# A layer's parameter loads issued one chunk sooner on SyncE, between the value transfers

## Chip, cores and metric
The kernel runs on one core of a Trainium2 chip. The metric is the device time of one execution in microseconds (us). The kernel before takes 7104.73 us, the median of three runs (7095.42 to 7106.72).

## What is computed
One sequence of 2048 tokens, 128 wide, in float32, passes four stages, each added to its input: causal attention with 16 heads of 8, a stack of 6 layers, grouped attention (16 query heads, 4 key groups of 64), and the same stack of 6 layers again with the same parameters. The change lies in the stack. One of its layers, cut to what matters:

```
def attn_layer(x, Wqkv, qs, ksc, Wo):          # 16 heads of 64, window 32
    q, k, v = split(x @ Wqkv)
    q = rotary(l2norm(q) * qs);  k = rotary(l2norm(k) * ksc)
    return local_attention(q, k, v) @ Wo
def ffn_layer(x, g, bln, W1, b1, W2, b2):      # hidden width 341
    xn = layernorm(x) * g + bln
    a, gate = split(xn @ W1 + b1)
    return a * gelu(gate) @ W2 + b2
for i in range(6):
    x = attn_layer(shift_tokens(x), Wqkv[i], q_scale[i], k_scale[i], Wo[i]) + x
    x = ffn_layer(shift_tokens(x), ln_g[i], ln_b[i], W1[i], b1[i], W2[i], b2[i]) + x
```

## The kernel before
A layer of the stack is worked through in 16 chunks of 128 tokens. The feed-forward part works on blocks of 4 chunks. Everything is one software pipeline: every engine runs a function `step` for k = 0 to 15 of each layer, and in one step it does different work for different chunks. On TensorE, step k holds the query and key projection of chunk k (L535 to L537), the value projection and the transposes of chunk k-1 (L542), the scores of chunk k-2 (a mask matmul, L704, then L711), the product of probabilities and values of chunk k-3 (L681), and the output projection of chunk k-4 with the weights `Wo` (L602). Block b enters the feed-forward part when its last chunk c = 4b+3 is through: the gate matmuls with `W1` (L546) run in step c+7, the three value matmuls with `W1` in steps c+8 to c+10 (each counted on `value_mm`), the matmuls with `W2` (L646) in step c+11. Within a step the order on TensorE is: normalisation and first value matmul, output projection (L602), gate matmul, transpose of the probabilities, `W2` matmuls, query projection, L681, L704 and L711, then the transposes and the value projection. The pipeline doesn't drain between layers: steps 0 to 11 of a layer still hold feed-forward work of the last block of the layer before.

Two steps follow from this for each layer's own parameters. `Wo` is last read for the layer before in step 3 (chunk 15) and first read for this layer in step 4 (chunk 0). `W1` is last read for the layer before in step 9 and first read for this layer in step 10. The biases `b1` of the value half are read by `hide` on VectorE (L1155) for the layer before until VectorE's step 10, and for this layer from its step 12. VectorE's step numbers run ahead of TensorE's: the product for this layer meets the chunk that TensorE has in step 11. Each parameter has one buffer, so its load waits until the last read of the layer before is done.

All these loads are issued by SyncE (SP), in program order, from `layer` in `sp_stack`. That function runs over the 16 chunks of a layer. For each chunk c it calls `window_values`, which waits until ScalarE has copied the values V of chunk c out of PSUM (L793, `v_sb`, at the end of TensorE's step c+1) and then issues ten transfers from `V` to `VW` (L456, L458, L460). They feed the L681 matmuls of chunk c, in step c+3. The parameter loads stand between these calls: each has the chunk c before whose `window_values` it is issued, and a wait on the semaphore of the last read. SP waits for both in the order in which they are written. Layer 0 of each call of the stack has its parameters loaded beforehand (`first`), so that the loads in question belong to 5 layers of each of the 2 calls, 10 in all. `load_wo` is one transfer (L422), `load_w1` one (L426), `load_b1` three (L436), `load_w2` three (L431), `load_cols` two (L441), `load_b2` one (L445) and `load_scales` six (L414, L417).

Of the kernel before, what the change touches and what calls it, by code (L numbers as in the profile page):

```python
# [90 lines left out]
def build(nc, A, out, place, stages=("A", "S0", "B", "S1")):  # L91
    n_const = A["shape_constants"].shape[1]
    ctx = ExitStack()
    with ctx:
# [303 lines left out]
        def sp_stack(sp, call):  # L398
            def load_q(layer):
                sp.dma_start(w_raw[0][:, :], A["Wqkv"][bass.ds(layer, 1), :, 0:INNER].rearrange("a p n -> p (a n)"))\  # L400
                  .then_inc(s["wqv_raw_in"], 16)

            def load_k(layer):
                sp.dma_start(w_raw[1][:, :], A["Wqkv"][bass.ds(layer, 1), :, INNER:2 * INNER]
                             .rearrange("a p n -> p (a n)")).then_inc(s["wk_raw_in"], 16)

            def load_v(layer):
                sp.dma_start(w_raw[0][:, :], A["Wqkv"][bass.ds(layer, 1), :, 2 * INNER:3 * INNER]
                             .rearrange("a p n -> p (a n)")).then_inc(s["wqv_raw_in"], 16)

            def load_scales(layer):
                for j, name in enumerate(("q_scale", "k_scale")):
                    row = A[name][bass.ds(layer, 1), :].rearrange("a n -> (a n)")
                    sp.dma_start(qk_scales[:, 2 * j, :], row.partition_broadcast(128))\  # L414
                      .then_inc(s["scales_in"], 16)
                    for x in range(2):
                        sp.dma_start(qk_scales[:, 2 * j + 1, 32 * x:32 * x + 32],  # L417
                                     row[32 - 32 * x:64 - 32 * x].partition_broadcast(128))\
                          .then_inc(s["scales_in"], 16)

            def load_wo(layer):
                sp.dma_start(Wo[:, :, :], A["Wo"][bass.ds(layer, 1), :, :].rearrange("a (j p) n -> p (a j) n", p=128))\  # L422
                  .then_inc(s["wo_in"], 16)

            def load_w1(layer):
                sp.dma_start(W1[:, :], A["W1"][bass.ds(layer, 1), :, :].rearrange("a p n -> p (a n)"))\  # L426
                  .then_inc(s["w1_in"], 16)

            def load_w2(layer):
                for j, (a, n) in enumerate(FT):  # L430
                    sp.dma_start(W2[0:n, j, :], A["W2"][bass.ds(layer, 1), a:a + n, :].rearrange("a p n -> p (a n)"))\  # L431
                      .then_inc(s["w2_in"], 16)

            def load_b1(layer, i):
                for j, (a, n) in enumerate(FT):
                    sp.dma_start(b1[0:n, i, j:j + 1], A["b1"][bass.ds(layer, 1), i * DFF + a:i * DFF + a + n]  # L436
                                 .rearrange("a p -> p a")).then_inc(s["gate_b_in" if i else "value_b_in"], 16)

            def load_cols(layer):
                for j, name in enumerate(("ln_g", "ln_b")):  # L440
                    sp.dma_start(ffn_cols[:, j:j + 1], A[name][bass.ds(layer, 1), :].rearrange("a p -> p a"))\  # L441
                      .then_inc(s["ln_cols_in"], 16)

            def load_b2(layer):
                sp.dma_start(ffn_cols[:, 2:3], A["b2"][bass.ds(layer, 1), :].rearrange("a p -> p a"))\  # L445
                  .then_inc(s["b2_in"], 16)

            def window_values(g, c):
                par = c % 2
                sp.wait_ge(s["v_sb"], START + g + c + 1)  # L450
                sp.sem_inc(s["passed"], 1)
                sp.wait_ge(s["pv_mm"], START + (max(g + c - 1, 0) if isinstance(g, int) else g + c - 1))
                for x in range(2):
                    cols = slice(512 * x, 512 * x + 512)
                    for w in range(1, 4):
                        sp.dma_start(VW[par][64 * x:64 * x + 64, w, :], V[par][32 * w - 32:32 * w + 32, cols])\  # L456
                          .then_inc(s["vs_in"], 16)
                    sp.dma_start(VW[par][64 * x:64 * x + 32, 0, :], V[1 - par][96:128, cols])\  # L458
                      .then_inc(s["vs_in"], 16)
                    sp.dma_start(VW[par][64 * x + 32:64 * x + 64, 0, :], V[par][0:32, cols])\  # L460
                      .then_inc(s["vs_in"], 16)

            def layer(L, following, after):
                first = isinstance(L, int) and L == 0
                g, f = L * NCH + CHUNKS * call, L * NB + BLOCKS * call
                t = (L + DEPTH * call) * 3
                if following is not None:
                    sp.wait_ge(s["w_lo_done"], START + t + 3)
                    load_q(following)
                for c in range(NCH):  # L470
                    if c == NCH - 1 and following is not None:
                        sp.wait_ge(s["w_lo_done"], START + t + 4)
                        load_v(following)
                        if after is not None:
                            sp.wait_ge(s["w_lo_done"], START + t + 5)
                            load_k(after)
                    if c == 3 and not first:
                        sp.wait_ge(s["y_mm"], START + g)
                        load_wo(L)
                    if c == 5:  # L480
                        sp.wait_ge(s["tables_done"], START + TABLES * call + 4 + 16 * L)
                        load_scales(0 if following is None else following)
                    if c == 7 and not first:
                        sp.wait_ge(s["ln_done"], START + norms_before(call) + f)
                        load_cols(L)
                    if c == 8 and not first:
                        sp.wait_ge(s["gelu_done"], START + 3 * f)
                        load_b1(L, 1)
                    if c == 9 and not first:
                        sp.wait_ge(s["value_mm"], START + 3 * f)  # L490
                        load_w1(L)
                    if c == 10 and not first:
                        sp.wait_ge(s["hid_done"], START + 3 * f)
                        load_b1(L, 0)
                    if c == 11 and not first:
                        sp.wait_ge(s["w2_mm"], START + f)
                        load_w2(L)
                    if c == 12 and not first:
                        sp.wait_ge(s["f_done"], START + 2 * f)
                        load_b2(L)  # L500
                    window_values(g, c)
# [21 lines left out]
        def norms_before(call):  # L523

            return (1 + (LN_S0 if call == 0 else LN_S1)) * NB - BLOCKS * call
# [1600 lines left out]
```

## Time and profile before
| | |
|---|---|
| time, median of 3 runs | 7104.73 us |
| the profiled execution: own time / span | 7119.09 / 7117.3 us |
| TensorE matmul busy / weight load busy | 6050.2 us (85%) / 4080.9 us (57%) |
| VectorE busy | 4642.6 us (65%) |
| GpSimd busy | 4252.9 us (60%) |
| ScalarE busy | 3318.6 us (47%) |
| mean granted TensorE clock over the span | 0.89 of full |

The times of the rows below come from the profiled execution. Its span runs from the first to the last instruction, and 1.8 us lie around it. A row of the timeline says when something started, how long it was busy, and in brackets how long its engine had been idle before it and what ended that idle time. The two calls of the stack lie at about 1040 to 3060 us and at about 5110 to 7117 us.

### The profile page before, as it was taken

The page shows a single profiled execution, that of the slowest core. Times are in us where ns is not written, and L with a number is a line of the kernel's source. Part 1 is how long each engine was busy: PE and PEld are TensorE (multiplying, and loading weights), DVE is VectorE, ACT ScalarE, POOL GpSimd, SP SyncE. Part 2 cuts the span into 40 slices and gives each one's busy share as a digit, 9 for nine tenths or more (in the row PEclk, how much of TensorE's full clock was granted, in tenths as well). Part 3 has the DMA queues.
Part 4 walks back from the last instruction along what each step waited for, and adds up shares of the span by engine and source line. Part 5 has one row for each costly group of instructions (what it writes and reads, how often), then busy time and mean ns, then how long its engine had stood idle before and what let it go on. Part 6 is the DMA issues. An engine that isn't in the chain of part 4 may idle for free. (4 is left out here: it accounts for less than half of the span.)

```text
span 7117.3 us, 188486 instructions
## 1 busy us (share of the span) xinstructions
PE 6050.2 (85%) x75387; PEld 4080.9 (57%) x75387; DVE 4642.6 (65%) x5380; ACT 3318.6 (47%) x3775; POOL 4252.9 (60%) x2000
## 2 busy tenths in 40 slices
PE   8989878888888888889889889999688888888887
PEld 4334436666666666655555555555376666666665
DVE  5425528887878887775455445543388787878776
ACT  1342246665656555513333333333366565656554
POOL 0000008777777777616567666667787777777764
PEclk6665569999999999989989989999899999999999
DMA  0000002222222222200000000000122222222221
GB/s 23 1 2 1 1 22 62 67 59 62 59 62 59 64 60 59 53 8 1 1 2 1 1 2 1 1 1 1 31 64 65 57 68 54 67 65 61 57 56 49
DMA packets 187287, 254.59 MB, mean 36 GB/s; under 512 B 59996, under 2 KB 80984, under 8 KB 186200
## 3 DMA queue, kind: packets, MB, share of 16 engines
q1 hardware_dynamic: 186392, 242.02, 13.1%
q8 instruction: 639, 10.47, 0.6%
q14 instruction: 256, 2.10, 0.1%
HBM read 38.98 MB, written 1.57 MB: 6 GB/s over the span
## 5 line engine op out<-in xcount | busy, mean ns | idle before, releaser
L1813 POOL TENSOR_TENSOR XB<-XB,Pb 128x1024 f32<-128x1024 f32 x448 | 1079.3, 2409 | 290.3 <-ACT Pb L1771 265.1
L913 POOL TENSOR_TENSOR sin_qk<-raw_qk,rot 128x512 f32<-128x512 f32 x768 | 1008.9, 1334 | 188.7 <-ACT raw_qk L875 133.1
L1865 DVE TENSOR_REDUCE b_pmax<-slot 128x1 f32<-128x1024 f32 x512 | 621.2, 1223 | 611.5 <-PE slot L1607 611.3
L1771 ACT ACTIVATE Pb<-slot 128x1024 f32<-128x1024 f32 x512 | 504.5, 1024 | 951.7 <-PE slot L1634 880.5
L946 POOL TENSOR_TENSOR inv_norm<-norm2c,minus_half 128x16 f32<-128x16 f32 x192 | 678.2, 3532 | 386.9 <-DVE norm2c L1088 386.9
L929 POOL TENSOR_TENSOR rot_out<-rot_out,sin_qk 128x1024 f32<-128x1024 f32 x192 | 601.2, 3131 | 337.7 <-DVE rot_out L987 336.6
L286 POOL TENSOR_TENSOR rstd<-variance,minus_half 128x4 f32<-128x4 f32 x20 | 19.8, 1008 | 1075.6 <-DVE variance L295 1075.5
L535 PE MATMUL slot<-w_hi,x_hi 128*128 128x512 f32 x1152 | 538.2, 467 | 73.5 <-POOL w_lo L904 43.4
L786 ACT ACTIVATE qT<-slot 128x1024 f32<-128x1024 f32 x192 | 197.1, 1026 | 794.3 <-PE slot L542 794.3
L942 POOL TENSOR_TENSOR inv_norm<-norm2c,minus_half 128x16 f32<-128x16 f32 x192 | 559.0, 2912 | 0.0
L987 DVE TENSOR_TENSOR rot_out<-slot,rot 128x1024 f32<-128x1024 f32 x384 | 467.9, 1219 | 83.5 <-PE slot L542 42.6
L711 PE MATMUL slot<-kT,qT 64*32 64x64 f32 x24576 | 334.6, 229 | 218.4 <-issue 218.3
L1644 PE MATMUL slot<-Pb,Vb 128*64 128x512 f32 x2048 | 494.3, 604 | 1.1 <-ACT Pb L1771 1.1
L542 PE MATMUL slot<-consts,rot_out 128*128 128x128 f32 x3072 | 435.1, 287 | 69.3 <-issue 39.5
L991 DVE TENSOR_TENSOR rot_out<-rot_out,inv_norm 128x1024 f32<-128x1024 f32 x384 | 474.9, 1237 | 6.8 <-POOL inv_norm L942 5.3
L602 PE MATMUL slot<-OT,Wo 128*128 128x128 f32 x3072 | 404.9, 288 | 82.7 <-DMA Wo<-in_Wo 80.0
L536 PE MATMUL slot<-w_lo,x_hi 128*128 128x512 f32 x1152 | 471.4, 409 | 2.6 <-issue 2.6
L537 PE MATMUL slot<-w_hi,x_lo 128*128 128x512 f32 x1152 | 469.6, 408 | 0.0
L711 PEld LDWEIGHTS slot<-kT,qT 64*32 64x32 f32 x24576 | 274.1, 107 | 325.9 <-issue 325.9
L602 PEld LDWEIGHTS slot<-OT,Wo 128*128 128x128 f32 x3072 | 386.5, 203 | 106.7 <-issue 101.8
L542 PEld LDWEIGHTS slot<-consts,rot_out 128*128 128x128 f32 x3072 | 363.8, 147 | 137.7 <-issue 84.0
L1632 PE MATMUL slot<-QA,KA 128*128 128x512 f32 x1024 | 423.6, 414 | 11.3 <-ACT Pb L1771 7.5
(223 smaller groups left out, 13525.8 us busy)
## 6 DMA issues: line engine op xcount, KB each, us to landing
VW<-V SPq DMA_DIRECT2D x1152, 128.0 KB
VW<-V SPq DMA_DIRECT2D x768, 64.0 KB
w_raw<-in_Wqkv SPq DMA_DIRECT2D x36, 512.0 KB, 3.6
Wo<-in_Wo SPq DMA_DIRECT2D x12, 512.0 KB, 4.1
W<-in_W SPq DMA_DIRECT2D x12, 341.0 KB, 3.1
consts<-in_shape_constants SPq DMA_DIRECT2D x1, 2436.5 KB, 8.7
W<-in_W SPq DMA_DIRECT2D x24, 64.0 KB
out<-out_nat SPq DMA_DIRECT2D x2, 512.0 KB, 3.4
```

The source lines that it names most:

```text
L535: pe.matmul(out, x_hi[ring][:, :], w_hi[:, cols], start=True, stop=False)
L542: mm = pe.transpose(o[:, j * 128:(j + 1) * 128], src[:, j * 128:(j + 1) * 128], ident)
L602: mm = pe.matmul(slot[2][:, 512:640], Wo[:, j, :], OT[:, j, :], start=(j == 0), stop=(j == 7))
L711: mm = pe.matmul(slot[3][32 * w:32 * w + 32, col:col + 64], qT[r:r + 64, h // 2, 32 * w:32 * w + 32], kT[r:r + 64, h // 2, 32 * w:32 * w + ...
L913: ins = pool.tensor_tensor(dst[:, :, x, :], src[:, :, 1 - x, :], tab, ALU.mult)
L929: pool.tensor_tensor(rot_out[0][:, :], rot_out[0][:, :], rot_sin[0], ALU.add)\
L942: pool.tensor_tensor(inv_norm[0][:, :], norm2c[0][:, :], minus_half[:, 0:H], ALU.pow)\
L946: pool.tensor_tensor(inv_norm[1][:, :], norm2c[1][:, :], minus_half[:, 0:H], ALU.pow)\
L1644: mm = pe.matmul(slot[3][64 * hh:64 * hh + 64, 0:512], Vb[:, k, :], Pb[:, n % B_RING, 512 * hh:512 * hh + 512], start=(k == 0), stop=(k == ...
L1771: act.activation(Pb[:, n % B_RING, :], slot[n % 2][:, :], ACT.Exp).then_inc(s["b_exp"], 1)
L1813: pool.tensor_tensor(b_sum[:, qb % 2, :], Pb[:, (n - 1) % B_RING, :] if k == 1 else b_sum[:, qb % 2, :], Pb[:, n % B_RING, :], ALU.add).th ...
L1865: dve.tensor_reduce(b_pmax[:, n // 2, n % 2:n % 2 + 1], o[:, :], AX.X, ALU.max).then_inc(s["b_max"], 1)
```

## The change
In `layer` eight conditions change. Each load that stood before the value transfers of chunk c now stands before those of chunk c-1. Their order among themselves, their waits and what they load stay the same. The loads of the projection weights (`load_q`, `load_v`, `load_k`) are not touched.

```diff
@@ -474,28 +474,28 @@
-                    if c == 3 and not first:
+                    if c == 2 and not first:
                         sp.wait_ge(s["y_mm"], START + g)
                         load_wo(L)
-                    if c == 5:
+                    if c == 4:
                         sp.wait_ge(s["tables_done"], START + TABLES * call + 4 + 16 * L)
                         load_scales(0 if following is None else following)
-                    if c == 7 and not first:
+                    if c == 6 and not first:
                         sp.wait_ge(s["ln_done"], START + norms_before(call) + f)
                         load_cols(L)
-                    if c == 8 and not first:
+                    if c == 7 and not first:
                         sp.wait_ge(s["gelu_done"], START + 3 * f)
                         load_b1(L, 1)
-                    if c == 9 and not first:
+                    if c == 8 and not first:
                         sp.wait_ge(s["value_mm"], START + 3 * f)
                         load_w1(L)
-                    if c == 10 and not first:
+                    if c == 9 and not first:
                         sp.wait_ge(s["hid_done"], START + 3 * f)
                         load_b1(L, 0)
-                    if c == 11 and not first:
+                    if c == 10 and not first:
                         sp.wait_ge(s["w2_mm"], START + f)
                         load_w2(L)
-                    if c == 12 and not first:
+                    if c == 11 and not first:
                         sp.wait_ge(s["f_done"], START + 2 * f)
                         load_b2(L)
                     window_values(g, c)
```

## Rows read from the trace of the kernel before

**Rows 1.** The page, part 1: busy time of each engine.
```profile
PE 6050.2 (85%) x75387; PEld 4080.9 (57%) x75387; DVE 4642.6 (65%) x5380; ACT 3318.6 (47%) x3775; POOL 4252.9 (60%) x2000
```

**Rows 2.** Waits of all engines: us in total, times, longest.
```profile
PE slot L602 <- DMA Wo<-in_Wo: 80.0, 10, 8.2
...
PE slot L546 <- DMA W<-in_W: 60.8, 10, 6.3
...
DVE normed L1155 <- DMA b<-in_b: 40.6, 10, 4.5
```

**Rows 3.** Waits of SP.
```profile
SPq L451 <- ACT V L793: 2360.9, 192, 22.8
```

**Rows 4.** Timeline, step 3 of layer 1, second call: start, us, engine.
```profile
5450.85 1.95 PE L602 MATMUL slot<-OT,Wo 128*128 128x128 f32 x16
5453.99 0.59 SPq L460 DMA_DIRECT2D VW<-V  x1
```

**Rows 5.** Timeline, step 4 of the same layer.
```profile
5466.78 1.95 SPq L456 DMA_DIRECT2D VW<-V  x3
...
5470.22 1.02 ACT L836 ACTIVATE kT<-slot 128x1024 f32<-128x1024 f32 x1
...
5473.46 0.40 SPq L422 DMA_DIRECT2D Wo<-in_Wo  x1
...
5477.56 3.53 PE L602 MATMUL slot<-OT,Wo 128*128 128x128 f32 x16 [8.20 <-DMA Wo<-in_Wo]
```

**Rows 6.** Timeline, steps 6, 9 and 10 of the same layer.
```profile
5515.88 1.88 PE L546 MATMUL slot<-normed,W 128*128 128x512 f32 x4
...
5574.31 1.35 SPq L436 DMA_DIRECT2D b<-in_b  x3
5574.60 1.02 PE L546 MATMUL slot<-normed,W 128*128 128x512 f32 x2
...
5580.13 0.74 DVE L1155 SCALAR_TENSOR_TENSOR normed<-slot,b,centred 128x512 f32<-128x512 f32 x1
...
5582.35 0.21 PE L711 MATMUL slot<-kT,qT 64*32 64x64 f32 x1 [2.25 <-issue]
...
5588.22 1.78 SPq L456 DMA_DIRECT2D VW<-V  x3
...
5595.09 0.35 SPq L426 DMA_DIRECT2D W<-in_W  x1
...
5598.15 3.78 PE L546 MATMUL slot<-normed,W 128*128 128x512 f32 x4 [6.34 <-DMA W<-in_W]
```

**Rows 7.** Timeline, step 11 of the same layer.
```profile
5623.91 1.37 SPq L436 DMA_DIRECT2D b<-in_b  x3
...
5627.17 0.75 DVE L1155 SCALAR_TENSOR_TENSOR normed<-slot,b,centred 128x512 f32<-128x512 f32 x1 [4.21 <-DMA b<-in_b]
```

**Rows 8.** Stretches L704 to L704: one step 4, sums of ten steps 4, 8, 12.
```profile
5459.18:5485.85 26.67, 17.00 (x334) 14.10 (x335) 18.10 (x21) 11.48 (x15) 14.46 (x8) 0.87 0.23 61
...
sum 277.51, PE 181.30 PEld 148.54 DVE 171.24 ACT 106.78 POOL 137.82; mean PE 18.13 PEld 14.85 DVE 17.12 ACT 10.68 POOL 13.78
...
sum 178.56, PE 158.81 PEld 128.78 DVE 167.01 ACT 115.74 POOL 135.42; mean PE 15.88 PEld 12.88 DVE 16.70 ACT 11.57 POOL 13.54
...
sum 181.97, PE 157.93 PEld 127.39 DVE 176.69 ACT 115.51 POOL 143.54; mean PE 15.79 PEld 12.74 DVE 17.67 ACT 11.55 POOL 14.35
```

**Rows 9.** The same view: sums of the ten steps 10, then of the ten steps 6.
```profile
sum 311.55, PE 223.17 PEld 155.34 DVE 198.84 ACT 141.40 POOL 190.28; mean PE 22.32 PEld 15.53 DVE 19.88 ACT 14.14 POOL 19.03
...
sum 217.28, PE 190.94 PEld 136.21 DVE 200.05 ACT 140.18 POOL 191.33; mean PE 19.09 PEld 13.62 DVE 20.00 ACT 14.02 POOL 19.13
```

**Rows 10.** The same view: sums of the ten steps 11, 7 and 15, in this order.
```profile
sum 218.76, PE 161.41 PEld 122.49 DVE 149.53 ACT 121.23 POOL 121.83; mean PE 16.14 PEld 12.25 DVE 14.95 ACT 12.12 POOL 12.18
...
sum 179.18, PE 153.30 PEld 120.22 DVE 152.38 ACT 119.98 POOL 125.42; mean PE 15.33 PEld 12.02 DVE 15.24 ACT 12.00 POOL 12.54
...
sum 186.45, PE 154.99 PEld 122.57 DVE 154.09 ACT 123.02 POOL 126.46; mean PE 15.50 PEld 12.26 DVE 15.41 ACT 12.30 POOL 12.65
```

## The prediction, made before the changed kernel was run
> **What bounds the kernel now.** I read the busy shares first: TensorE's matmuls fill 85% of the span, VectorE 65%, GpSimd 60% [rows 1]. So TensorE is the engine whose idle time is worth finding, and there isn't much of it. Next I read the list of waits and looked for those that end with a transfer, since the change moves only transfers. Three end with a parameter load: TensorE's output projection waits 80.0 us for `Wo`, its gate matmul 60.8 us for `W1`, and VectorE's product L1155 40.6 us for the biases `b1` [rows 2]. Each occurs ten times, once in each of the five later layers of both calls, and the longest is hardly above the mean (8.2 against 8.0, 6.3 against 6.1, 4.5 against 4.1), so it is a fixed cost of a layer. The other parameters (`W2`, scales, norm columns, `b2`, the gate half of `b1`) have no such wait.
>
> The timeline shows why. In step 4 SP issues the ten value transfers of chunk 2 from 5466.78 on and only then, at 5473.46, the load of `Wo`. TensorE wanted it at 5477.56 - 8.20 = 5469.36 [rows 5]. But the last read of the old `Wo` was over at 5450.85 + 1.95 = 5452.80 [rows 4]. So the buffer lay free for 20 us while SP stood at its wait for the next values; SP spends 2360.9 us on that wait in all [rows 3]. Step 10 repeats it for `W1` (issued 5595.09, wanted 5598.15 - 6.34 = 5591.81), and step 11 for `b1` (issued from 5623.91, wanted 5627.17 - 4.21 = 5622.96) [rows 6, 7].
>
> **What these stalls cost.** The wait isn't all. After the idle time the sixteen L602 matmuls take 3.53 us instead of 1.95 [rows 4, 5], and the four L546 3.78 us instead of 1.88 [rows 6]: twice the time, the 1.2 GHz level of the granted clock instead of 2.4, and the granted mean of that step 4 is 0.87 [rows 8]. So I took the cost from whole steps, since the pipeline's work repeats with k modulo 4. A stretch runs from one L704 to the next.
> - Ten steps 4 take 277.51 us. Ten steps 8 take 178.56, ten steps 12 take 181.97 [rows 8]. Excess 95.5 to 99.0 us.
> - Ten steps 10 take 311.55 us, ten steps 6 217.28 [rows 9]. Excess 94.3 us. Part of it isn't the stall: the step shown has a 2.25 us idle ahead of L711 that no transfer ended [rows 6]. From the single stall, 6.34 us of wait and 3.78 - 1.88 = 1.90 us of slow matmuls make 8.2 us, 82 us for ten. I take 82 and keep 94 for the range.
> - Ten steps 11 take 218.76 us, ten steps 7 179.18, ten steps 15 186.45 [rows 10]. Excess 32.3 to 39.6 us; I take 36, the middle. This wait is VectorE's; TensorE feels it through the sum `XB` (L1067), which stands behind L1155 on VectorE.
>
> **The change part by part.**
> *`Wo`, chunk 3 to 2.* SP is through with the transfers of chunk 1 at 5453.99 + 0.59 = 5454.58, later than the last read (5452.80), so its wait on `y_mm` costs nothing. The load is issued at about 5454.9 and lands after 4.1 us (now 5473.46 to 5477.56), at 5459.0: 10.4 us before it is wanted [rows 4, 5]. Next late in step 4 would be the transpose of the probabilities, which needs ScalarE's copy L836, done at 5471.24 [rows 5]. The output projection would end at about 5469.36 + 1.95 = 5471.3, with one more matmul after it, so that copy isn't late either. Gain 95.5 us.
> *`W1`, chunk 9 to 8.* The old `W1` is free when the third value matmul is through, 5574.60 + 1.02 = 5575.62. SP will wait there about 1.5 us, since the transfers of chunk 7 are out by 5574.31, where the gate biases are issued now. Queued behind this wait on SP are the ten value transfers of chunk 8, which can't start before 5588.22 anyway. The load lands at 5575.7 + 3.1 = 5578.8 and is wanted at 5591.81: 13 us spare [rows 6]. Without the stall step 10 is a step 6, in which VectorE is busy for 20.0 of 21.7 us [rows 9]: near its bound, but not over. Gain 82 us.
> *`b1`, value half, chunk 10 to 9.* The new place is that of `W1` now, 5595.09. Its last read, L1155 in step 10, is over at 5580.87, so there is no wait. Landing takes 5627.17 - 5623.91 = 3.3 us, so it is there at 5598.4, 24.6 us early [rows 6, 7]. Gain 36 us.
> *The other fifteen transfers* (six scales, two norm columns, three gate biases, three `W2`, one `b2`) go one step sooner. Their waits are for reads that lie at least a step back, and the step has SP idle most of the time [rows 3]. Nobody waits for them now, so they gain nothing. Their price: between 0 and what a load could take from TensorE's instruction supply, priced below. I take 0, because their number and sizes stay the same and nothing is queued behind them on SP until the next chunk's values.
> Nothing is added to or taken from VectorE, ScalarE, GpSimd or TensorE.
>
> The sum is 95.5 + 82 + 36 = 213.5 us. Against the profiled execution (7119.09 us) that is 6905.6; the median of the runs stands 14.4 us lower, and the change is costed on it: 7104.7 - 213.5 = 6891.
>
> The Trainium skill, "TensorE: Matmul & The Clock Gate", section "What's actually happening", says that "the default state is throttled, and activity releases the throttle". By this the slow matmuls vanish with the idle time, as the sum has it. Without it only the waits would come back. The trace agrees, in that the slow groups stand directly behind the stalls [rows 5, 6].
>
> **The rivals.**
> *Only the waits come back.* If the slow stretches only move elsewhere, or VectorE, at 20.0 of 21.7 us in such steps, takes them, the gain is the waits alone: 80.0 + 60.8 + 40.6 = 181.4 us, 6923 us; if VectorE's wait is off the path too, 140.8 us, 6964. For it: the tight VectorE. Against it: the partner steps have the same work and are shorter by the full amount. 18%.
> *The loads delay the value transfers.* The Trainium skill, "DMA: Bandwidth & Descriptors", section "Queues, rings and completion order", says that on each DMA engine descriptors are consumed in ring order, so that a load issued first is ahead of the next value transfers. No row here shows two transfers holding each other up. As a mechanism of this kernel: if TensorE's L681 waited for values held up by the three loads, each would give back its landing time, 4.1 + 3.1 + 3.3 = 10.5 us, 105 us for ten layers, leaving 6996 us. Against it: `Wo` would land at 5459.0 and the next value transfer is issued at 5466.78; `W1` at 5578.8 against 5588.22 [rows 5, 6]. 3%.
> *The loads starve TensorE's instruction supply: slower.* TensorE idles without a releaser in most steps, and the 2.25 us ahead of L711 in step 10 follow the load of the gate biases at 5574.31 by 6 us [rows 6]. If each of the eight groups of loads in its new place cost such an idle time more, it would be 8 x 10 x 2.25 = 180 us, and the time 7071. It becomes slower than before when each costs over 213.5 / 80 = 2.7 us; at 3 us it is 240 us, 7131 us. Against it: these loads have been there all along, one step later, in steps with the same work. 3%.
> *The change doesn't do what it says.* If one of the waits were satisfied only a step later, as a semaphore count could have it, its load would stay where it is; for all three nothing changes, 7105 us. Against it: the last reads are in the rows, 2 us before and 1.5 us after SP gets there. 3%.
>
> **How the numbers follow.** The forecast, all three stalls gone with their slow matmuls, has 70%, and its own range is 6872 to 6905: the lower end is 99.0 + 94.3 + 39.6 = 232.9 us gained, the upper 200. More than that, because slow stretches in the steps after the stalls vanish too, has 3%. The rivals have 18, 3, 3 and 3%. The range goes from 6860, a little below the largest excess, to 6965, where both of TensorE's waits come back and nothing else. Faster by over 0.2% (about what a measurement can tell from no change): 70 + 3 + 18 + 3 = 94%. Within 0.2%: 3%. Slower: 3%.
>
> **What would show each step.** The three rows of waits for `Wo`, `W1` and `b1` should be gone. Ten steps 4 should sum to about 182 us, ten steps 10 to about 230, ten steps 11 to about 183. `Wo` should be issued right behind the value transfers of chunk 1, `W1` right behind the third value matmul. TensorE's busy time should fall by some 60 us (18.13 - 15.88, 22.32 - 19.09 and 16.14 - 15.33 us, ten times each [rows 8 to 10]), and the mean granted clock should rise above 0.89. The prediction is wrong if a new wait of L681 for `VW` appears, or if idle time without a releaser ahead of L711 grows by more than 2 us a step, or if VectorE's waits vanish while the steps stay long.

## The result

The changed kernel takes 6911.4 us, the median of four runs (6898.31 to 6924.76), against 7101.05 us before in the runs beside it. The ratio is 0.9733 with an interval of 0.9712 to 0.9754: 190 us, or 2.7%, faster. The profiled execution of it took 6912.81 us with a span of 6911.0 us.

Two terms return below. The granted clock is the share of TensorE's full clock that it was given in a stretch. Idle time without a releaser is idle time for which the profile shows nothing that was waited for (`issue` in the rows); the prediction put it down to TensorE's instruction supply, that is, to instructions arriving late.

The page of the changed kernel, part 1 (busy time of each engine, answering to [rows 1]) and the start of part 4 (the chain of waits):

```profile
PE 6008.5 (87%) x75387; PEld 4065.0 (59%) x75387; DVE 4643.1 (67%) x5380; ACT 3318.6 (48%) x3775; POOL 4250.3 (61%) x2000
...
PE 17%; issue 4%; DVE 3%; ACT 2%; SPq 1%; POOL 1%; DMA 0%; DVEq 0%; ACTq 0%; POOLq 0%
```

TensorE's busy time fell by 41.7 us and its share rose from 85% to 87%. In the chain the share of transfers (DMA) went from 1% to 0%. The three waits of [rows 2] are gone from the list. SP has one new wait in their place, the one foreseen for the third value matmul before the load of `W1`. The waits of SP in the changed kernel:

```profile
SPq L451 <- ACT V L793: 2147.8, 192, 21.8
...
SPq L426 <- PE slot L546: 11.6, 10, 1.7
```

It holds SP for 1.2 us a layer, and nobody waits for that. SP waits 213 us less for V; the spans differ by 206 us, so most of that is simply the shorter pipeline.

The timeline of layer 1, second call, in the changed kernel, answering to [rows 4 to 7]: start, duration, engine, and in brackets the idle time before.

```profile
5353.15 1.95 PE L602 MATMUL slot<-OT,Wo 128*128 128x128 f32 x16
...
5357.15 0.40 SPq L422 DMA_DIRECT2D Wo<-in_Wo  x1
...
5371.55 2.03 PE L602 MATMUL slot<-OT,Wo 128*128 128x128 f32 x16
...
5396.56 0.35 PE L681 MATMUL slot<-VW,probsT 64*32 64x64 f32 x17 [1.84 <-issue]
...
5472.47 0.35 SPq L426 DMA_DIRECT2D W<-in_W  x1
...
5488.23 1.88 PE L546 MATMUL slot<-normed,W 128*128 128x512 f32 x4
...
5491.65 1.69 SPq L436 DMA_DIRECT2D b<-in_b  x3
...
5510.59 0.75 DVE L1155 SCALAR_TENSOR_TENSOR normed<-slot,b,centred 128x512 f32<-128x512 f32 x1 [0.23 <-issue]
```

`Wo` is issued 14.4 us before the output projection that needs it, `W1` 15.8 us before the gate matmuls, and `b1` 18.9 us before the product. The sixteen L602 take 2.03 us instead of 3.53, the four L546 1.88 instead of 3.78: behind the vanished stalls of this layer TensorE runs at the 2.4 GHz level (its step 4 has a granted clock of 1.00; in the first call it is 0.81 to 1.00). One kind of row is new: 1.84 us of idle time without a releaser ahead of L681, in step 5.

The stretches from L704 to L704 give the balance. The stretch called step k begins with the L704 of step k-1, so that the scores (L711) at its start are those of step k-1, and those of step k fall into the next. These are the sums of the ten steps 4, 10 and 11 of the changed kernel (total us, busy time of each engine, then the means), against 277.51, 311.55 and 218.76 us in [rows 8 to 10]:

```profile
sum 172.04, PE 157.94 PEld 128.95 DVE 156.15 ACT 106.83 POOL 125.91; mean PE 15.79 PEld 12.90 DVE 15.61 ACT 10.68 POOL 12.59
...
sum 231.06, PE 201.99 PEld 148.08 DVE 194.65 ACT 141.28 POOL 188.45; mean PE 20.20 PEld 14.81 DVE 19.46 ACT 14.13 POOL 18.85
...
sum 179.26, PE 152.59 PEld 119.50 DVE 149.72 ACT 119.58 POOL 122.01; mean PE 15.26 PEld 11.95 DVE 14.97 ACT 11.96 POOL 12.20
```

The steps 4 lost 105.5 us, the steps 10 80.5, the steps 11 39.5: 225.5 us together, more than the 213.5 foreseen. But the spans differ by 206.3 us only. So some of it came back, and the largest part of that in the two steps behind step 4. The twenty steps 5 and 6, first of the kernel before, then of the changed one:

```profile
sum 384.88, PE 344.68 PEld 261.53 DVE 326.65 ACT 250.92 POOL 335.10; mean PE 17.23 PEld 13.08 DVE 16.33 ACT 12.55 POOL 16.75
...
sum 410.25, PE 361.82 PEld 278.39 DVE 336.61 ACT 251.00 POOL 341.32; mean PE 18.09 PEld 13.92 DVE 16.83 ACT 12.55 POOL 17.07
```

They grew by 25.4 us. What grew is TensorE's idle time without a releaser, from 1.4 to 3.3 us in the mean of the five steps 6 of the first call. The experiments are about this. Theory A: the scales' six loads, which moved from the end of step 6 to the end of step 5, hold up TensorE's instruction supply. Theory B: the stall for `Wo` gave the supply time to catch up, and without it the idle time shows wherever the loads stand.

### The profile page after: what moved, and what is told of

Same layout as the page of the kernel before. It is cut to its first block and busy times, and to the rows that moved or that the text cites. A ratio compares the mean times of both kernels' runs of the same rounds, so it can differ in the third digit from the quotient of the medians.

```text
span 6911.0 us, 188486 instructions
## 1 busy us (share of the span) xinstructions
PE 6008.5 (87%) x75387; PEld 4065.0 (59%) x75387; DVE 4643.1 (67%) x5380; ACT 3318.6 (48%) x3775; POOL 4250.3 (61%) x2000
## 3 DMA queue, kind: packets, MB, share of 16 engines
q8 instruction: 639, 10.47, 0.6%
## 5 line engine op out<-in xcount | busy, mean ns | idle before, releaser
L711 PE MATMUL slot<-kT,qT 64*32 64x64 f32 x24576 | 338.6, 232 | 226.3 <-issue 226.3
L711 PEld LDWEIGHTS slot<-kT,qT 64*32 64x32 f32 x24576 | 277.2, 108 | 334.5 <-issue 334.5
L1634 PE MATMUL slot<-QB,KB 66*128 66x512 f32 x1024 | 415.7, 406 | 0.0
L602 PE MATMUL slot<-OT,Wo 128*128 128x128 f32 x3072 | 388.0, 281 | 2.7 <-ACT OT L814 2.7
```

Source lines behind the costliest of these rows:

```text
L711: mm = pe.matmul(slot[3][32 * w:32 * w + 32, col:col + 64], qT[r:r + 64, h // 2, 32 * w:32 * w + 32], kT[r:r + 64, h // 2, 32 * w:32 * w + ...
```

## Experiments

Unless said otherwise an experiment differs from the kernel before by what its diff shows, which is cut to the lines that matter. Ratios are to the runs of the kernel before beside it, with the interval in brackets. A gain in us is worked out from the ratio; the interval is some 13 to 16 us to either side, and the plain difference of the medians lies up to 8 us off. What one kernel does more than another is therefore read from the steps wherever the times are close.

### Only Wo moved
```diff
-                    if c == 3 and not first:
+                    if c == 2 and not first:
                         sp.wait_ge(s["y_mm"], START + g)
                         load_wo(L)
```


> Only the load of Wo moves, from chunk 3 to chunk 2. The changed kernel shortened the ten steps 4 by 105 us but lengthened steps 5 and 6 by 25 us, by idle time of TensorE without a releaser. Theory A (the scales' six loads, now at the end of step 5, hold up TensorE's instruction supply): the scales stay here, so steps 5 and 6 stay as before and the time is 7101 - 105 = 6996 us. Theory B (the 8 us stall for Wo gave the instruction supply time to catch up, and without it the idle time shows in the next steps, wherever the loads stand): steps 5 and 6 grow by 25 us, 7021 us.

Measured: 7018.97 us, ratio 0.9880 (0.9858 to 0.9902), 85 us faster. The sum of its ten steps 4, then of its twenty steps 5 and 6:

```profile
sum 175.67, PE 160.72 PEld 131.78 DVE 157.01 ACT 106.72 POOL 125.49; mean PE 16.07 PEld 13.18 DVE 15.70 ACT 10.67 POOL 12.55
...
sum 389.76, PE 350.09 PEld 266.98 DVE 338.98 ACT 250.68 POOL 342.80; mean PE 17.50 PEld 13.35 DVE 16.95 ACT 12.53 POOL 17.14
```

Step 4 loses 101.8 us. Steps 5 and 6 give back 4.9 us, not 25. It lies in step 5 of the second call (89.59 against 84.16 us for five), where 1.3 to 1.6 us of idle time ahead of L681 appear in four of the five layers that show none before. So theory B holds for a fifth of the effect, in one place, and A is left for the rest. The time itself came out nearer to B's 7021 than to A's 6996, against what the steps say. I go by the steps, since the two times lie hardly further apart than the interval.

### Only the scales moved
```diff
-                    if c == 5:
+                    if c == 4:
                         sp.wait_ge(s["tables_done"], START + TABLES * call + 4 + 16 * L)
                         load_scales(0 if following is None else following)
```


> Only the scales' six transfers move, from chunk 5 to chunk 4; nobody waits for them in either place. Theory A: steps 5 and 6 grow by about 25 us together (idle ahead of L711 in step 6 of the first call, ahead of L681 in step 5 of the second), 7126 us, unless the stall for Wo one step earlier absorbs part. Theory B: no difference, 7101 us.

Measured: 7139.59 us, ratio 1.0046 (1.0028 to 1.0064): 33 us slower than before (20 to 46 by the interval), by a load for which nobody waits. Steps 5 and 6 together grow by 21.4 us (384.88 to 406.24), here in step 6 of both calls. (The profiled execution was the fastest of the four, 7110.55 us; its other steps happen to be shorter than those in the profile of before. So the 33 us rest on the medians; the steps show the place and 21 us of it.) The rows of L711 in step 6, layer 3 of the first call, with the idle time ahead of them, and the last scale transfers ahead of them; first the kernel before, which issues them after this row:

```profile
2111.06 0.97 PE L711 MATMUL slot<-kT,qT 64*32 64x64 f32 x73 [1.18 <-issue]
...
2124.55 0.86 SPq L417 DMA_DIRECT2D qk_scales<-in_q_scale  x2
```

With only the scales moved:

```profile
2098.86 0.34 SPq L414 DMA_DIRECT2D qk_scales<-in_q_scale  x1
...
2101.15 0.86 SPq L417 DMA_DIRECT2D qk_scales<-in_k_scale  x2
2105.03 1.34 PE L711 MATMUL slot<-kT,qT 64*32 64x64 f32 x73 [2.83 <-issue]
```

The idle time stands in the middle of a group of matmuls that all have their operands. It grew from 1.18 to 2.83 us, and the 73 matmuls behind it take 1.34 us instead of 0.97, since TensorE's clock fell too (0.86 granted in this step, 1.00 before). This is theory A with the stall for `Wo` still in place, so that B can't be its cause.

### The changed kernel with the scales put back
```diff
@@ against the changed kernel
-                    if c == 4:
+                    if c == 5:
                         sp.wait_ge(s["tables_done"], START + TABLES * call + 4 + 16 * L)
                         load_scales(0 if following is None else following)
```


> The changed kernel with the scales' load put back before chunk 5. Theory A: steps 5 and 6 return to their lengths of before, 6911 - 25 = 6886 us. Theory B: no difference, 6911 us.

Measured: 6888.87 us, ratio 0.9695 (0.9677 to 0.9714): 3.05% faster than before, and 27 us (0.9733 - 0.9695) better than the changed kernel, with both intervals some 20 us to either side; the medians differ by 22.5 us. Steps 5 and 6 take 389.63 us, as with `Wo` alone. The part 1 of its page:

```profile
PE 5980.6 (87%) x75387; PEld 4040.2 (59%) x75387; DVE 4643.1 (67%) x5380; ACT 3320.0 (48%) x3775; POOL 4256.9 (62%) x2000
```

TensorE's busy time is down by 69.6 us here, where the changed kernel had 41.7: the idle times at the start of step 6 had cost clock as well. This version is faster than both kernels.

### Only the three loads that were waited for
```diff
-                    if c == 3 and not first:
+                    if c == 2 and not first:
                         sp.wait_ge(s["y_mm"], START + g)
                         load_wo(L)
...
-                    if c == 9 and not first:
+                    if c == 8 and not first:
                         sp.wait_ge(s["value_mm"], START + 3 * f)
                         load_w1(L)
-                    if c == 10 and not first:
+                    if c == 9 and not first:
                         sp.wait_ge(s["hid_done"], START + 3 * f)
                         load_b1(L, 0)
```


> Only the three loads that somebody waited for move (Wo, W1, value half of b1); the other fifteen transfers stay. Theory A: the full 225 us that steps 4, 10 and 11 lost, with nothing given back at steps 5 and 6: 7101 - 225 + some 5 for W1's own neighbourhood = 6880 us. Theory B: 25 us of it are given back, 6905 us.

Measured: 6891.4 us, ratio 0.9697 (0.9678 to 0.9716); steps 5 and 6 take 391.90 us. It equals the run before it, which moves nine transfers more (norm columns, gate biases, `W2`, `b2`). So of the fifteen transfers that nobody waited for, the six scales alone had a price, and the nine others none that shows within the interval.

### Only W1 moved
```diff
-                    if c == 9 and not first:
+                    if c == 8 and not first:
                         sp.wait_ge(s["value_mm"], START + 3 * f)
                         load_w1(L)
```


> Only the load of W1 moves, from chunk 9 to chunk 8. The ten steps 10 lose their stall and its slow matmuls, 80 us; the wait for b1 in step 11 stays. The time is 7105 - 80 = 7025 us. If TensorE's instruction supply had lived on this stall (theory B) the steps behind would give back as much as step 5 does behind the stall for Wo, some 5 us; if the load of W1 at the end of step 9 holds the supply up as the scales' loads do (theory A), idle time ahead of L711 in step 10 of the first call grows by 1 us a step, as it did in the changed kernel.

Measured: 7027.06 us, ratio 0.9870 (0.9850 to 0.9890), 92 us faster. Its ten steps 10:

```profile
sum 226.18, PE 194.61 PEld 139.72 DVE 199.08 ACT 141.84 POOL 190.68; mean PE 19.46 PEld 13.97 DVE 19.91 ACT 14.18 POOL 19.07
```

85.4 us less than before. The steps behind give nothing back, so this stall wasn't cover for the instruction supply. Nor does step 10 of the first call show the 1 us of idle time that theory A allowed for the load of `W1`: five of them take 109.5 us, nearly as the steps 6 there do (108.6). In the changed kernel the same five take 114.0 us, and with the three loads alone 109.6, so this growth isn't due to `W1`; no run says what it is due to.

### Only the value half of b1 moved
```diff
-                    if c == 10 and not first:
+                    if c == 9 and not first:
                         sp.wait_ge(s["hid_done"], START + 3 * f)
                         load_b1(L, 0)
```


> Only the three transfers of the value half of b1 move, from chunk 10 to chunk 9. They now stand behind the load of W1, which is as late as before. If VectorE's wait of 4.1 us a layer is on the path, the ten steps 11 become 39 us shorter and the time is 7105 - 39 = 7066 us; if it was cover for something else, less. TensorE's instruction supply may take a few us at steps 11 and 12 instead.

Measured: 7084.5 us, ratio 0.9946 (0.9928 to 0.9965), 38 us faster. Its ten steps 11 take 183.33 us instead of 218.76, 35.4 us less. VectorE's wait of 4.1 us a layer (40.6 us in all) was on the path for the most part. The three gains, 1.20%, 1.30% and 0.54%, add up to 3.04%; the three loads together gave 3.03%. Within the intervals the stalls are independent of each other. The steps agree: 101.8, 85.4 and 35.4 us one by one make 222.6, and with the three loads together the same steps lose 226.9.

### The changed kernel with the scales loaded twice
```diff
@@ against the changed kernel; load_spare is load_scales into squares[:, 1, :]
                         load_scales(0 if following is None else following)
+                        load_spare(0 if following is None else following)
```


> The changed kernel, in which the six scale transfers before chunk 4 are issued a second time, into a part of a tile (squares) that the stack doesn't use. Half of the six (the run with the scales split) cost as much idle time as all six. If TensorE's supply is held until the last of these transfers has landed, six more (some 3.3 us of issuing) lengthen the idle ahead of L711 in step 6 of the first call from 3.4 us to about 6.7, 30 us more for ten layers, 6941 us. If the presence of such a load is what counts, the idle stays at 3.4 us and the time at 6911. Theory B: 6911.

Measured: 6923.21 us, ratio 0.9730 (0.9708 to 0.9753), the same as the changed kernel. In step 6 of the first call the idle time doesn't grow (2.8 to 3.9 us, against 2.8 to 3.6 in the changed kernel), and five of these steps take 120.29 us against 120.30. In the second call, where the first six had lengthened step 5, the further six are issued across the beginning of step 6 and lengthen that one: ahead of L711 there are 3.0 to 4.3 us of idle time, where the changed kernel has 0.6 to 1.7. Steps 5 and 6 together take 421.74 us, 11.5 more than in the changed kernel. The span of this execution is 9.2 us longer (6920.2 against 6911.0), but that is no proof of the 11.5: its other steps of the stack were 17 us shorter and the parts outside the stack 15 us longer. So the first six transfers have their price whatever follows them, and the further six cost 2.3 us in each of the five layers of the second call, where they come to lie across one more such place. Each place at which the supply runs short while such loads are in flight costs some 2 us, once.

### The changed kernel with the scales split over two chunks
```diff
@@ against the changed kernel, shortened; load_scales is given which of the two scales it loads
                     if c == 4:
-                        load_scales(0 if following is None else following)
+                        load_scales(0 if following is None else following, (0,))   # q_scale: three transfers
+                    if c == 5:
+                        load_scales(0 if following is None else following, (1,))   # k_scale: the other three
```


> The changed kernel with the three transfers of the query scales before chunk 4 and the three of the key scales before chunk 5. Theory A by number: half of the 22 us comes back, 6900 us. If it is only the last transfers, which lie nearest to the instruction fetch, that hold it up, all of it comes back, 6889 us. Theory B: 6911 us.

Measured: 6919.4 us, ratio 0.9715 (0.9696 to 0.9734). The ratio lies midway between the changed kernel and the one with the scales put back and decides nothing; the steps do. Step 6 of layer 3, first call:

```profile
2062.68 0.96 SPq L419 DMA_DIRECT2D qk_scales<-in_q_scale  x2
2069.19 0.97 PE L715 MATMUL slot<-kT,qT 64*32 64x64 f32 x73 [3.10 <-issue]
```

Three transfers cost nearly as much as six: steps 5 and 6 take 408.09 us, against 410.25. Both forms of theory A that went by number or by the last transfer are out.

### Another load in the scales' place
```diff
@@ against the kernel with the scales put back
+                    if c == 4:
+                        sp.dma_start(squares[:, 1, :], A["Wqkv"][bass.ds(L, 1), :, 0:512].rearrange("a p n -> p (a n)"))\
+                          .then_inc(s["spare_in"], 16)
```


> The kernel with the scales back before chunk 5 (6889 us), and one other load before chunk 4 in their place: 256 KB in rows of 2 KB from the projection weights, into a part of a tile (squares) that the stack doesn't use. If any load in that place holds up TensorE's instruction supply, the idle ahead of L711 in step 6 of the first call is 3.4 us as in the changed kernel, and the time is about 6911. If it takes the small broadcast rows of the scales, the idle stays at 1.4 us and the time at 6889.

Measured: 6906.82 us, ratio 0.9713 (0.9690 to 0.9736). The time lies between the two cases and its interval touches both. The steps decide: steps 5 and 6 take 391.12 us, like the 389.63 without this load and unlike 410.25. The row:

```profile
2049.77 0.44 SPq L481 DMA_DIRECT2D squares<-in_Wqkv  x1
2054.72 0.97 PE L714 MATMUL slot<-kT,qT 64*32 64x64 f32 x73 [1.45 <-issue]
```

A load of 256 KB in rows of 2 KB, issued in the same place, leaves the idle time at the start of step 6 of the first call nearly where it was: 1.3 to 2.0 us in the five layers. In the second call it doesn't. There the idle time ahead of L681 in step 5 is 1.6 to 2.3 us, as in the changed kernel (1.6 to 2.7) and above the 1.2 to 1.6 us that four of these layers have with the scales put back (the fifth has none), and the five steps 5 take 94.85 us against 95.21 in the changed kernel and 89.71 with the scales put back. Only the steps 6 behind them make up for it: 103.4 us, against 107.6 with the scales put back. So this load holds up the supply too, in one of the two places.

The scales come as transfers of 32 and 16 KB, in rows of 256 and 128 bytes that are broadcast to all partitions. It is tempting to say that it takes the small rows or the broadcast, but there is a third difference, time. In the first call the 256 KB have landed 0.4 to 0.8 us behind the L704 that opens step 6; of the scales' six transfers the first lands 0.9 to 1.8 us behind it and the last 4.7 to 5.2 (2.7 to 4.4 with three). The large load may be harmless there because it is over sooner. The runs don't tell the three apart.

## Why the prediction was right, and where it wasn't

*The three stalls, their places and their length.* Right. The loads are issued where it was said (`Wo` behind the transfers of chunk 1, `W1` 1.2 us after SP is ready), the waits are gone, and no new wait of L681 for `VW` came in their place (2.4 us in all, 2.8 before).

*Cost by whole steps rather than by waits.* Right. The waits are 181.4 us, the sum was 213.5, the steps lost 225.5. Term by term: `Wo` 95.5 foreseen, 105.5 measured, `W1` 82 and 80.5, `b1` 36 and 39.5. The undersized term is `Wo`: the partner steps 8 and 12 are themselves a little longer than a step 4 without its stall (17.9 and 18.2 us in the mean against 17.2). The rival "only the waits come back" is out: with the three loads alone moved the kernel gains 3.03%, some 215 us. The changed kernel's own time couldn't have told: its 190 us lie nearer to the rival's 181.4 than to the sum's 213.5, and its 6911.4 us outside the 6872 to 6905 that the prediction gave its own forecast (whose upper end, 200 us gained, it doesn't work out; its low terms add up to 209.8). What made the difference is the next term.

*The other fifteen transfers at 0.* Here the step failed. "Their number and sizes stay the same and nothing is queued behind them on SP" was no reason, because what they met wasn't on SP. Six of them, the scales, cost 27 us in the changed kernel and 33 us alone by the times, and 20.6 and 21.4 us by the steps 5 and 6. The mechanism had been named among the rivals, with 2.25 us as the price of one such meeting, and that is about the size measured (idle time of 1.4 us that became 3.3 in step 6 of the first call, over 2 us more in two of the five layers, which the prediction had named as a sign of being wrong). But it was priced for all eight groups of loads or none, and set aside because "these loads have been there all along". That overlooks that a load's neighbours change when it moves. Whether a load meets a moment at which TensorE needs instructions depends on where in the step it lies, and the scales moved from a harmless place into a harmful one.

*The give-back behind the stall.* The other 5 of the 25.4 us that steps 5 and 6 gave back, in step 5 of the second call, went to the instruction supply once the stall for `Wo` was gone. The sum had nothing for it. 225.5 less 25.4 is 200.1 us, and the spans differ by 206.3; the 6 us between are spread over the rest, and one execution of each kernel doesn't attribute them. The medians differ by 190 us only, since the profiled execution of before, at 7119.09 us, was slower than the median of its runs.

*TensorE's busy time.* About 60 us less was foreseen and 41.7 came, and the mean granted clock rose from 0.890 to 0.895 only (0.900 with the scales put back); 17 us of busy time came back in steps 5 and 6 (361.82 - 344.68), where matmuls behind the new idle times ran slow.

*How the scales lengthen the idle time.* The traces show one link more. The page of this kernel lists a queue of the kind `instruction` with 639 packets of 16 KB, 10.47 MB in all (q8), and the trace has the time of each packet. In the kernel before, TensorE has 184 idle times of over 0.9 us without a releaser in the two calls of the stack (from the first L704 of each to its last), and every one of them ends 1.2 to 2.0 us (1.4 in the median) behind the end of such a packet; in the changed kernel it is the same for all 182. So these are waits for instructions. At step 6 of the first call the packet in question starts between 0.05 us ahead of and 0.26 us behind the L704 that opens the stretch. In the changed kernel it starts 1.9 to 2.7 us behind it, with only the scales moved 1.9 to 2.8, with three transfers 2.1 to 2.6, with twelve 1.9 to 2.9, and with the other load 0.2 to 1.1. The packet before it is as early as ever (6.7 to 7.1 us ahead of L704, as before), and the late packet takes no longer than before (0.9 to 1.0 us, against 1.1 to 1.5). What the scales do is make this packet start some 2 us later.

The Trainium skill, "Runtime: NRT & Kernel Launch", section "Instruction fetch mechanics", says that each engine's sequencer fetches its next instructions over a DMA queue of its own while it executes. That fits this queue. What stays open is what holds the packet's start back. TensorE goes on 6.1 to 7.7 us after the first scale transfer is issued, in step 6 of the first call, whether three, six or twelve are issued, so the packet doesn't wait for all of them; that it waits behind those that were issued before it was asked for is possible, and no trace here shows when it was asked for.

## What to carry to other kernels

In this kernel a load that TensorE waited for once in every layer was worth its wait plus the slow matmuls behind it, and the cheapest way to size it is to compare whole steps with their partners. Move only the loads that somebody waits for: in this kernel the three that mattered gave 3.03% by themselves, and moving the six scale transfers with them took 0.4% away. Before you move a load "for free", look for idle time without a releaser on the busiest engine in the step that it moves into, and for an `instruction` queue on the page.

## Not expected of the hardware

Six broadcast loads with rows of 128 to 256 bytes, in flight while TensorE is in the middle of a group of ready matmuls, lengthened its idle time without a releaser from 1.4 to 3.3 us (means of the five steps 6 of the first call). Three such loads did as much (3.1 to 3.7 us), and twelve no more in that place (2.8 to 3.9 us). The traces show where the growth comes from: the packet of instructions that ends this idle time started some 2 us later. A load of 256 KB in rows of 2 KB cost little there (1.3 to 2.0 us), and about as much as the scales in step 5 of the second call.

The effect is tied to the moment and not to a fixed place of the program: with the scales alone moved it shows in step 6 of both calls. In the changed kernel the second call has the first scale transfer issued 4.9 to 5.7 us ahead of the L704 that opens step 6, instead of 3.0 to 3.6, and there it shows mostly in step 5 (11.0 us for the five, against 3.3 in step 6).
